# Attention and mixture-of-experts layer on one core: two neighbouring exponentials of each head group computed by one 128x2048 instruction

## The reference, cut to what matters

```python
scores = jnp.einsum('bhqd,bhkd->bhqk', q, k) / jnp.float32(np.sqrt(HD))
amask = jnp.where((j >= i - W) & (j < i), jnp.float32(-10000000000.0), jnp.float32(0.0))
attn = jax.nn.softmax(scores + amask[None, None, :, :], axis=-1)
out = jnp.einsum('bhqk,bhkd->bqhd', attn, v).reshape(Bb, Ll, Dm)
```

## Time and profile before

| | us |
|---|---|
| median of 3 runs | 905.71 |
| the profiled execution's own time | 906.11 |
| its span in the trace | 904.4 |
| PE busy | 870.5 (96%) |
| ACT busy | 578.6 (64%) |
| DVE busy | 450.7 (50%) |
| POOL busy | 276.2 (31%) |
| 336 plain exponentials, L958 | 319.9 |
| 112 merged and mixed ones, L969 | 112.4 |

### The profile page before, as it was taken

One profiled execution on the slowest core, in us unless ns is written; L12 is line 12 of the kernel. 1 busy time (PEld: TensorE's weight loads), 2 busy tenths in 40 slices (PEclk: granted clock), 3 DMA queues, 4 the chain that ended last, 5 costly groups with the idle time before them and its releaser, 6 DMA issues.

```text
span 904.4 us, 22574 instructions
## 1 busy us (share of the span) xinstructions
PE 870.5 (96%) x8167; PEld 561.6 (62%) x8168; DVE 450.7 (50%) x776; ACT 578.6 (64%) x733; POOL 276.2 (31%) x423
## 2 busy tenths in 40 slices
PE   8989999999999999999999999999999999999994
PEld 5524444433434343343447888888888989999983
DVE  8644443344444334454548677667834343434332
ACT  4789999999999999999993433342222222222220
POOL 5043334333333433333340000000024454544442
PEclk9979999999999999999999999999999999999998
DMA  6345444665544466733102206100037875575421
GB/s 189 122 132 185 151 164 164 218 214 210 193 154 162 161 219 228 244 99 90 31 13 76 70 27 240 50 1 24 1 101 217 269 226 160 158 205 154 121 36 23
DMA packets 42062, 124.43 MB, mean 138 GB/s; under 512 B 7668, under 2 KB 23028, under 8 KB 35824
## 3 DMA queue, kind: packets, MB, share of 16 engines
q1 hardware_dynamic: 31152, 110.35, 35.9%
q0 software_dynamic: 7072, 9.72, 6.0%
q10 hardware_dynamic: 3744, 3.02, 1.0%
HBM read 74.03 MB, written 49.02 MB: 136 GB/s over the span
## 4 chain that ended last, share of the span: by engine, by line
PE 79%; ACT 13%; issue 4%; DVE 2%; DMA 1%; POOL 0%; ACTq 0%; POOLq 0%; DVEq 0%
PE ps L1737 18%; PE ps L1910 14%; PE ps L1690 13%; PE ps L1864 12%; ACT arena L958 12%; PE ps L1932 7%; PE ps L1877 6%; PE ps L1921 2%; PE ps L1631 2%; PE ps L1791 2%; PE ps L1891 1%; DMA out<-arena,now_to 0%; PE ps L1821 0%; DMA xres<-x 0%; PE ps L1851 0%
## 5 line engine op out<-in xcount | busy, mean ns | idle before, releaser
L958 ACT ACTIVATE arena<-ps 128x1024 f32<-128x1024 f32 x336 | 319.9, 1063 | 2.0 <-PE ps L1690 2.0
L1737 PE MATMUL ps<-arena 128*32 128x256 f32 x4096 | 265.6, 386 | 0.6 <-POOL arena L785 0.6
L785 POOL TENSOR_SCALAR_AFFINE_SELECT arena<-arena 128x512 f32<-128x512 f32 x240 | 150.1, 638 | 265.7 <-ACT arena L969 258.0
L1690 PE MATMUL ps<-arena 64*128 64x512 bf16 (+1 forms) x1280 | 176.9, 343 | 12.1 <-ACT arena L958 8.5
L1737 PEld LDWEIGHTS ps<-arena 128*32 128x32 f32 x4096 | 112.4, 110 | 99.1 <-issue 42.4
L1690 PEld LDWEIGHTS ps<-arena 64*128 64x128 bf16 x1280 | 57.7, 94 | 157.9 <-ACT arena L958 79.5
L1189 DVE COPY_PREDICATED ps<-keep,ps 128x512 f32<-128x512 int32 (+1 forms) x128 | 80.6, 629 | 143.8 <-PE ps L1690 143.8
L1910 PE MATMUL ps<-wr_all,x2T 128*128 x648 | 141.3, 362 | 2.0 <-issue 1.0
L1910 PEld LDWEIGHTS ps<-wr_all,x2T 128*128 128x128 f32 x648 | 106.7, 189 | 19.5 <-issue 4.1
L1864 PE MATMUL ps<-x2T,wr_all 128*128 128x512 f32 x480 | 116.8, 394 | 1.3 <-issue 1.2
L969 ACT ACTIVATE arena<-ps 128x1024 f32<-128x1024 f32 x112 | 112.4, 1062 | 0.5 <-PE ps L1690 0.4
(11 more groups left out here) (198 smaller groups left out, 706.1 us busy)
## 6 DMA issues: line engine op xcount, KB each, us to landing
w_scr<-wr_all SPq DMA_DIRECT2D x24, 1280.0 KB, 7.3
wr_all<-w_scr SPq DMA_DIRECT2D x24, 1280.0 KB, 6.1
raw<-w_experts SPq DMA_DIRECT2D x24, 640.0 KB, 7.8
arena<-q_scr SPq DMA_DIRECT2D x64, 64.0 KB
o_scr<-arena SPq DMA_DIRECT2D x128, 32.0 KB, 1.7
arena<-o_scr SPq DMA_DIRECT2D x16, 256.0 KB, 4.0
raw<-w_shared SPq DMA_DIRECT2D x6, 640.0 KB, 5.0
q_scr<-parts SPq DMA_DIRECT2D x8, 384.0 KB, 3.0
```

The costliest lines, as they stand in the source:

```text
L785: nc.gpsimd.affine_select(out=dst, in_=src, compare_op=ALU.is_ge if own else ALU.is_gt, fill=0.0, base=0, pattern=[[0, REP], [-1 if own el ...
L958: nc.scalar.activation(prob[:, SLOT[unit(a, kt)], :, :].rearrange("p h q -> p (h q)"), score.rearrange("p b x -> p (b x)"), ACT.Exp, scale ...
L1690: return nc.tensor.matmul(ps[:, bank, :].rearrange("p (h q) -> p h q", h=2)[:, :, place * P:(place + tiles) * P], kst[r0:r0 + HALF, s, kt ...
L1737: last = nc.tensor.matmul(ps[32 * h:32 * h + 32, 6 + qc, a % 2 * QW:(a % 2 + 1) * QW], vst[:, s, kt, :], prob[:, SLOT[k], h, :], start=(no ...
```

## The change

Exponentials 26 and 27 of each group (plain units (3,2) and (3,3), which lie in neighbouring buffers 0 and 1 and go to neighbouring ring slots 8 and 9) become one ScalarE instruction on 128x2048 values. It waits for both S26 and S27, and adds 2 to `s_free` when it is done. Everything that waits for E26 now waits for the pair (`END_OF`). The condition on which an S waits for its buffer is also written in another way: it names the exponential at place i-3 of TensorE's own order `ISSUE`, through the new function `freed_by`.

```diff
+TWIN = {e: e + 1 for e in (26,)}
+END_OF = {e: e + (e in TWIN) for e in range(NEXP)}
...
+def freed_by(e):
+
+    i = ISSUE_NO[e]
+    return (0, END_OF[ISSUE[i - BUFS]]) if i >= BUFS else (1, END_OF[ISSUE[i - BUFS + NEXP]])
...
     if kt in plain_of(a):
-        return EXPS.index((PLAIN, a, kt))
+        return END_OF[EXPS.index((PLAIN, a, kt))]
...
                 for e, (kind, a, kt) in enumerate(EXPS):
-                    for k in slots_written(e):
+                    if e - 1 in TWIN:
+                        continue
+                    both = [e, e + 1] if e in TWIN else [e]
+                    for k in [k for one in both for k in slots_written(one)]:
...
-                        act.wait_ge(s_ready, n * NEXP + (ISSUE_NO[e] + 1))
+                        act.wait_ge(s_ready, n * NEXP + (max(ISSUE_NO[one] for one in both) + 1))
                     score = ps[:, 2 * BUF[e]:2 * BUF[e] + 2, :]
-                    if kind == PLAIN:
+                    if len(both) == 2:
+                        slot = SLOT[unit(a, kt)]
+                        assert SLOT[unit(a, EXPS[e + 1][2])] == slot + 1
+                        nc.scalar.activation(prob[:, slot:slot + 2, :, :].rearrange("p c h q -> p (c h q)"),
+                                             ps[:, 2 * BUF[e]:2 * BUF[e] + 4, :].rearrange("p b x -> p (b x)"), ACT.Exp,
+                                             scale=SCALE).then_inc(s_free, 2)
+                    elif kind == PLAIN:
...
-                pe.wait_ge(s_free, n * NEXP + (i + 1))
                 e = ISSUE[i]
+                back, before_it = freed_by(e)
+                pe.wait_ge(s_free, n * NEXP + (BUFS - NEXP * back + before_it + 1))
```

More of the change, by code:

```diff
@@ L111 @@
 NEXP = len(EXPS)
+TWIN = {e: e + 1 for e in (26,)}
+END_OF = {e: e + (e in TWIN) for e in range(NEXP)}
+assert all(EXPS[e][0] == EXPS[e + 1][0] == PLAIN and EXPS[e][1] == EXPS[e + 1][1] for e in TWIN)
 TURNS = (((3, 4), ((3, 4, 1), (3, 5, 1), (0, 3))),
@@ L152 @@
 BUF = buffers()
+assert all(BUF[e + 1] == BUF[e] + 1 for e in TWIN)
+def freed_by(e):
+    i = ISSUE_NO[e]
+    return (0, END_OF[ISSUE[i - BUFS]]) if i >= BUFS else (1, END_OF[ISSUE[i - BUFS + NEXP]])
 def slot_of_unit(k):
```

## The result

The changed kernel takes **926.54 us** (median of 4 runs, 925.48 to 926.91), the kernel before 905.74 (4 runs). The ratio is 1.023, with a 95% interval of 1.0217 to 1.0243: slower by 20.8 us, where 19.4 had been forecast (925.1).

The account below looks back on a forecast made before the run. The prediction saw a lockstep of two nearly full engines, ScalarE and TensorE. Per group 0.18 + 1.03 = 1.21 us, times 16 groups 19.4 us, on the median of 905.71 gave 925.1 us, range 919.0 to 929.5.

Parts of the forecast that it names:

- S9: Its rewritten wait is for one exponential more, which ends at 401.79; ScalarE idles 0.18 us.
- S14 to E2': Lateness per group from S14's wait to the next group's exponential 2: 1.03 us, with 0.10 and the pair's 0.08 in it.
- S14 to E20: S14 would wait for one exponential more; work behind moves 0.23, E18 comes late through VectorE's merge, 0.10 us stays.
- S25: Right behind S24 on TensorE, it would wait for E23 and move from 415.26 to 416.27, by 1.01 us.
- The pair waits for S27: S27 moves from 417.24 to 418.25, so the pair starts 0.95 us later than E26 did.
- The pair's duration: Length of the joined 128x2048 exponential on ScalarE: taken as 1.85 us, between 1.77 and 1.96.
- S0' 0.05 after the pair: Next group's first S on TensorE waits for the pair's end and starts 0.05 us after it.
- The rewritten waits cost nothing: Rival: S25's wait is free and only the pair counts, 1.3 us, giving 907.0; chance 0.06.
- The pair's gain arrives: Rival: S1' comes before 419.84 with waits as before, at most 2.4 us faster, giving 903.3; chance 0.03.
- The clock: Rival: TensorE loses its clock in the new idle times, some 5 us per group, about 1005 us; chance 0.03.

Follow-up runs that it names:

- E26: Not a run: exponential 26 of a group on ScalarE, a single in the kernel before; it started at 417.79 in the 14th group.
- E16: Not a run: exponential 16 of a group on ScalarE.
- E18: Not a run: exponential 18 of a group on ScalarE, forecast to come 0.23 us late.
- E17: Not a run: exponential 17 of a group on ScalarE; it started at 409.42 in the kernel before.
- E23: Not a run: exponential 23 of a group on ScalarE; it ended at 416.12 in the kernel before.
- load_wait_ahead: Pair with old waits, but the wait for the group's loads moved from S0' to S28, against exact_waits: 907.68 us, ratio 1.0021 to the kernel before.
- exact_waits: Changed kernel with the pair kept and every S again waiting for the last exponential that used its buffer: 908.96 us, ratio 1.0038 to the kernel before.
- waits_only: Changed kernel without the pair, only the rewritten waits: 920.28 us, ratio 1.0166 to the kernel before.
- E28: Not a run: exponential 28 of a group on ScalarE, which follows the pair.
- v_ahead_alone: Kernel before, without pair and with its own waits, V(3,7) moved ahead of S1': 904.58 us, ratio 0.9991.
- s0_late: Kernel before, with the next group's S0' waiting for exponential 27 in place of 26: 910.25 us, ratio 1.0047.
- E8: Not a run: exponential 8 on ScalarE, the only one of its size in a group, from whose starts the period is read.
- two_singles: exact_waits with the pair as two 128x1024 instructions that wait together and release together: 909.9 us, ratio 1.0048 to the kernel before.
- E1': Not a run: exponential 1 of the next group on ScalarE.

## Why the prediction was right

**Which term, and its size.** The sum was 0.18 (S9) + 1.03 (S14 to E2') = 1.21 us per group; the steady groups show 1.32. From E9 to the start of the pair it is 16.58 us in place of 15.64 (to E26), 0.94 late with 0.95 forecast; from there to E2' it is 4.92 in place of 4.73, 0.19 late with 0.08 forecast. So nearly all of the miss lies behind the pair's start. By its steps:

- *S9* "moves to 401.84, E9 to 402.33", 0.18 late: 0.71 - 0.53 = 0.18 in the changed kernel. Alone it measures 2.4 us, 0.15 per group; the period rises by 0.12, so a little less arrives than the 0.18. What takes up the rest was not followed.
- *S14 to E20*, 0.10 left over: the start of E20 is 3.92 us behind that of E16 in the changed kernel (425.56 to 429.48), and 412.35 - 408.52 = 3.83 before, so 0.09; counted from E9 it is 10.26 against 10.20, 0.06. Right in size, but not in the whole path: the prediction had E18 late by VectorE's merge, and in the changed kernel E17, which waits for no merge, already starts 1.08 us after E16 (426.64 - 425.56), 0.18 late. S14 was not tried alone.
- *S25* moves by 1.01 and waits for E23: it does, 0.06 after its end, with TensorE idle 0.77 us (0.6 forecast). The term is the largest also when it is taken away alone (13.7 us).
- *The pair waits for S27*: from E25's start at 434.00 to the pair's at 435.80 it is 1.80 us where one step is 0.90, so ScalarE loses 0.90 us, 0.85 forecast.
- *The pair's duration*, taken at 1.85: 1.88 where it followed an idle time, 1.94 where it didn't. The estimate that was set beside it, 1.89 by the Trainium skill, "ScalarE: Activation LUTs", What ACT_TABLE_LOAD costs, is the better one for the changed kernel.
- *S0' 0.05 after the pair*: this is the reading that was wrong. It starts 0.14 to 0.15 after (435.80 + 1.88 = 437.68 to 437.83). The 0.05 had been read from S1', which waits for one semaphore; S0' waits for two. It is worth 0.09 us per group; load_wait_ahead costs 1.4 us less than exact_waits, each taken against the kernel before on its own chip.

0.09 and 0.03 (1.88 for 1.85) are 0.12 us per group, about what the steady groups are longer than forecast (1.32 for 1.21). That the time misses by 1.4 us and not by 1.8 is the difference between the mean of all groups and the steady ones.

**The rivals.** "The rewritten waits cost nothing" falls with waits_only. "The pair's gain arrives" falls with exact_waits: even with the old waits the pair costs 3.4 us, two and a half times the 1.3 that the prediction gave it: S0' 0.09 later, and a pair of 1.94 in place of 1.85. The clock stayed at 1.00 in the 14th group, with TensorE idle for 1.74 us of 27.66. That rival called a mean of 0.52 "half the time and more at 1.2 GHz"; it is nearly the whole stretch at 1.2 GHz, and its price of 5 us in 10 goes by that.

**What the pair is worth.** Where TensorE has something to do under it, the kernel with the pair is 1.2 us faster than the one without (903.38 and 904.58, measured on the same chip), 0.08 us per group by the medians and 0.09 by the mean periods; the saved start on ScalarE alone, 2 x 0.90 - 1.75 (from the pair's start at 393.83 to E28's at 395.58 in exact_waits), is 0.05. In steady groups the period is 26.25 without the pair and 26.18 with it, a difference of 0.07. The rest lies in single groups: in the kernel before, in v_ahead_alone and in s0_late, the same three groups (9th, 11th and 15th, counted from E8 to E8) are 0.06 to 0.3 us longer than the others, and with the pair, and in two_singles too, they are not. What holds ScalarE there is not known, so the 1.2 us are not all the pair's saved start. Of the versions that were run, the pair with old waits and one or two V moved is faster than the kernel before, by 0.2 to 0.3%. That the moved V pays is clear with the pair, and at the edge of what can be told without it.

## What to carry to other kernels

A wait written for "who had this buffer last" must name the tenant by the same order by which the buffers were given out; two orders that differ in four swapped places cost 14.7 us here. Joining two instructions of a full engine saves one start, 0.05 us for this pair, and releases the first one's buffer one whole instruction later: look first at what the other engine did in that time, and give it work that waits for neither. When two engines run in lockstep, a part of the time won at one wait is given back at the next (3.0 us expected, 2.2 and 1.0 won), so follow the chain for several steps ahead before counting a gain 16 times.

## What the runs showed of the hardware

An S that waited for ScalarE alone started 0.05 to 0.06 us after it, and one that also waited for the loads' semaphore, long fulfilled, 0.14 to 0.15. It was there in the changed kernel, exact_waits, two_singles and s0_late, and went when that wait was moved. In the trace, one of two waits on a matmul is an instruction of its own (EVENT_SEMAPHORE, 0.05 us) ahead of the weight load, and here it was the one for ScalarE.

The duration of an exponential of the same size depends on what stood before it: 1.02 us behind an idle time, and longer with each neighbour that follows without one, up to 1.12 (E1' in exact_waits), while the starts stay 0.90 apart. It is the end that releases a buffer, so in a run without holes the releases come up to 0.1 us later than the first duration lets one expect. The pair shows the same, 1.88 and 1.94 us.
